# Mixture-of-experts tiles of seven sequences in one queue, with blocks that wait until they are full

## The reference, cut to what matters

```python
m = _layernorm(x, ln2_g, ln2_b)                     # x: 4096 tokens x 128
probs = softmax(m @ Wg)                             # E = 8 experts
wts, idx = top_k(probs, 2); wts = wts / sum(wts)
h1 = gelu(einsum('td,edf->etf', m, W1) + b1)        # F = 512
ye = einsum('etf,efd->etd', h1, W2) + b2
out = x + sum_k wts[k] * ye[idx[k]]                 # each token uses 2 of 8 experts
```

## Time and profile before

| | us |
|---|---|
| timed runs, three | 1022.54, 1027.51 (median), 1029.69 |
| span of the profiled execution, first to last instruction | 987.7 |
| the profiled execution's own time | not given; the median stands for it |
| PE busy | 820.5 (83%) |
| VectorE busy | 665.6 (67%) |
| ScalarE busy | 600.2 (61%) |
| GpSimd busy | 424.9 (43%) |

### The profile page before, as it was taken

One profiled execution on the slowest core, in us unless ns is written; L12 is line 12 of the kernel. 1 busy time (PEld: TensorE's weight loads), 2 busy tenths in 40 slices (PEclk: granted clock), 3 DMA queues, 4 the chain that ended last, 5 costly groups with the idle time before them and its releaser, 6 DMA issues. The chain is left out here.

```text
span 987.7 us, 15981 instructions
## 1 busy us (share of the span) xinstructions
PE 820.5 (83%) x5416; PEld 516.9 (52%) x5416; DVE 665.6 (67%) x1341; ACT 600.2 (61%) x1016; POOL 424.9 (43%) x543
## 2 busy tenths in 40 slices
PE   3558898878898999788989998988898888898772
PEld 1444445434555654345556555654565555478771
DVE  4538858886879688868886878687867576223112
ACT  2123446644787687447876887677768876556341
POOL 5544333534553455464534553454556013115263
PEclk9675798888899999898999999998999998699797
DMA  6500321991522300015233321053223320558793
GB/s 196 169 12 9 122 98 49 292 347 45 179 90 89 101 21 9 12 33 180 89 100 103 108 86 57 30 183 97 89 80 123 119 80 27 181 188 298 236 309 95
DMA packets 106286, 116.77 MB, mean 118 GB/s; under 512 B 7983, under 2 KB 89310, under 8 KB 106206
## 3 DMA queue, kind: packets, MB, share of 16 engines
q1 hardware_dynamic: 102110, 107.36, 34.3%
q0 software_dynamic: 4096, 8.40, 2.6%
HBM read 77.24 MB, written 38.49 MB: 117 GB/s over the span
## 5 line engine op out<-in xcount | busy, mean ns | idle before, releaser
L1456 DVE TENSOR_REDUCE QA<-psB 128x2 f32<-128x1024 f32 x256 | 311.9, 1219 | 124.0 <-PE psB L1143 121.7
L943 ACT ACTIVATE PT<-psB 128x1024 f32<-128x1024 f32 x256 | 261.9, 1023 | 134.3 <-PE psB L1159 130.4
L1159 PE MATMUL psB<-Q,KT 32*128 32x512 f32 x512 | 134.4, 521 | 34.0 <-ACT PT L943 20.6
L1143 PE MATMUL psB<-KT,Q 24*128 24x512 f32 x512 | 136.9, 530 | 22.6 <-DVE QA L1456 21.7
L1171 PE MATMUL psV<-PT,VA 128*32 128x512 f32 x1024 | 148.5, 654 | 0.6
L1236 PE MATMUL psA<-MX,WB 128*128 128x128 f32 x792 | 109.4, 290 | 31.2 <-ACT H L971 19.7
L971 ACT ACTIVATE H<-psA,WB 128x128 f32<-128x128 f32 x396 | 109.8, 376 | 33.3 <-PE psA L1236 31.3
L1236 PEld LDWEIGHTS psA<-MX,WB 128*128 128x128 f32 x792 | 100.0, 202 | 39.4 <-issue 28.3
L1246 PEld LDWEIGHTS psY<-WB,H 128*128 128x128 f32 x792 | 96.8, 194 | 27.8 <-ACT H L971 16.8
L1159 PEld LDWEIGHTS psB<-Q,KT 32*128 32x128 f32 x512 | 49.7, 191 | 117.1 <-ACT PT L943 75.3
L1246 PE MATMUL psY<-WB,H 128*128 128x128 f32 x792 | 107.6, 282 | 0.0
(11 more groups left out here) (198 smaller groups left out, 1360.0 us busy)
## 6 DMA issues: line engine op xcount, KB each, us to landing
WB<-w_rows SPq DMA_DIRECT2D x99, 578.0 KB, 5.7
pairs<-XT SPq DMA_DIRECT2D x2, 5120.0 KB, 18.5
outs<-XT SPq DMA_DIRECT2D x2, 5120.0 KB, 33.5
XT<-pairs SPq DMA_DIRECT2D x99, 64.0 KB
outs<-YT SPq DMA_DIRECT2D x99, 64.0 KB
w_rows<-WB SPq DMA_DIRECT2D x8, 578.0 KB, 3.3
X<-in_L_attn_x_dram SPq DMA_DIRECT2D x8, 256.0 KB, 3.0
H<-in_L_ffn_W_dram SPq DMA_DIRECT2D x8, 256.0 KB, 3.9
```

What stands on the lines that cost most here:

```text
L943: act.activation(PT[:, (c % 2) * G + j:(c % 2) * G + j + 2, :], psT, ACT.Exp, scale=SCALE).then_inc(t_taken.sem, 1)
L1143: pe.matmul(dst[:, h, :], chunk(Q1[r, g, :], c), KT[r, g, :], start=True, stop=True).then_inc(s_full.sem, 1)
L1159: pe.matmul(psT[:, h, :], chunk(KT[r, g, :], c), Q2[r, g % 2, :], start=True, stop=True).then_inc(t_full.sem, 1)
L1456: dve.tensor_reduce(QA[:, c, g * G + j:g * G + j + 2, RM], plain(b, i), AX_X, ALU.max).then_inc(s_taken.sem, 1)
```

## The change

- Elements 0 to 6 form one group and element 7 the other. A group has *stages*: after each element from the second on, a stage runs the tiles whose blocks are full for certain (128 rows); unfilled blocks wait for later elements, and the last stage of a group takes all that is left. Seven stages with 9, 8, 8, 8, 8, 22, 15 tiles: 78 instead of 99. Windows: 3, 3, 3, 3, 3, 8, 5.
- Stages begin at slots 88, 120, 152, 184, 216, 248, 280. Windows start 8 slots apart, in the last two stages 4 apart (248 to 276 and 280 to 296); there the third W1 step stands half a slot later.
- `tile_map` looks at up to 224 blocks, keeps the flags of the stage before and takes the difference; 10 instructions (8 or 9 in a group's first stage) instead of 6; it runs after elements 1 to 7.
- A row in `XS` has 130 columns. The scatter writes 129 of them, with the pair's place in the result at one end. VectorE reads it back from the loaded tile (`tile_places`, slot 4 of a window) and waits there until the store of the window before last has landed.
- The result is stored straight in token order (`TK`), by GpSimd with an indirect DMA a tile, at slot 11 of a window. The gathers go. SyncE fetches the results of an element in two plain DMAs of 256 KB into one buffer for each choice, each once the combine before has freed it.
- Combines and output stores of elements 0 to 6 all come behind the last window of their group: fetches at slots 288, 290, ... 300, combines at 290, 292, ... 302; element 7 at 308 and 310. The sum X1 + Z1 is kept in XZ, which now holds eight elements.
- `XS` is cleared in eight pieces, one a turn, with 17 MB in all; four areas with 20.5 MB were cleared before. `YS` needs no clearing.

```diff
-    MEMBERS = [[0]] + [[b, b + 1] for b in range(1, B - 1, 2)] + [[B - 1]]
+    MEMBERS = [list(range(B - 1)), [B - 1]]
...
+            known = 2 * T // TW * (i + 1) + (E - 1 if b == m[-1] else 1 - E)
+            if i or b == m[-1]:
+                STAGE[b] = len(TILES)
+                TILES.append(known - given)
...
-        STRIDE = [8, 8, 8, 5, 8]
+        STRIDE = [8] * (STAGES - 2) + [4, 4]
...
             def rows_in(w):
...
                 if w >= 2:
                     u = use(members(w - 2)[0], "x")
                     sp.wait_ge(u.taken, u.after)
+                    sp.wait_ge(places.sem, places.at(w - 2, 1))
...
+            def fetch_rows(b):
+                if b == MEMBERS[GROUP_OF[b]][0]:
+                    for w in range(LAST_WINDOW[GROUP_OF[b]] - 1, LAST_WINDOW[GROUP_OF[b]] + 1):
+                        sp.wait_ge(y_out[w % 2], moved(w))
+                for k in range(2):
+                    if b > 0:
+                        sp.wait_ge(*((combined.sem, combined.at(b - 1, 1)) if k else (dve_y, b)))
+                    first = (k * B + b) * T
+                    sp.dma_start(YG[:, k, :, :], TK[first:first + T, :].rearrange("(c p) n -> p c n", p=P)).then_inc(fetched[k], 16)
...
-            TILE = {3: (tile_step(0, next_rows),), 7: (tile_step(0, next_weights),), 9: (tile_step(0, rows_out),)}
+            TILE = {3: (tile_step(0, next_rows),), 7: (tile_step(0, next_weights),)}
+            END = {4: (fetch(0),), 6: (fetch(1),), 8: (fetch(2), keep(0),), 10: (fetch(3), keep(1),), 12: (fetch(4), keep(2),),
+                   14: (fetch(5), keep(3),), 16: (fetch(6), keep(4),), 18: (keep(5),), 20: (keep(6),)}
...
-                            pool.indirect_dma_start(XS[GROUP_OF[b] % 2], bass.IndirectOffsetOnAxis(IDX[:, b % 6, k, c:c + 1], 0),
-                                                    ZM[:, b % 2, c, :], None).then_inc(scattered[k][c], 16)
+                            pool.indirect_dma_start(XS.rearrange("r n -> (r n)").unsqueeze(1), bass.IndirectOffsetOnAxis(IDX[:, b % 2, k, c:c + 1], 0),
+                                                    ZM[:, b % 2, c, k:k + C + 1], None).then_inc(scattered[k][c], 16)
...
+            def tile_out(first):
+                w = window(first)
+                pool.wait_ge(places.sem, places.at(w, 1))
+                pool.wait_ge(y_taken.sem, y_taken.at(w, 1))
+                for i in range(len(members(w))):
+                    pool.indirect_dma_start(TK, bass.IndirectOffsetOnAxis(IDT[:, w % 2, i:i + 1], 0),
+                                            YT[:, w % 2, i, :], None).then_inc(y_out[w % 2], 16)
+
+            TILE = {11: (tile_step(0, tile_out),)}
...
             POST = {6: (c_norm,), 16: (positions, scatter(0),), 21: (scatter(2),)}
-            END = {4: (gather(0, 0),), 8: (gather(0, 1), gather(0, 2),), 16: (gather(0, 3),), 17: (gather(1, 0),),
-                   31: (gather(1, 1),), 32: (gather(1, 2), gather(1, 3),)}
...
+            def tile_places(first):
+                w, size = window(first), len(members(window(first)))
+                dve.wait_ge(xt_in[w % 2], moved(w))
+                if w >= 2:
+                    dve.wait_ge(y_out[w % 2], moved(w - 2))
+                own_p.begin(w)
+                own_p.link(dve.tensor_tensor(IDF[:, 0:size], XT[:, w % 2, 0:size, 0], XT[:, w % 2, 0:size, C + 1], ALU.min))
+                own_p.end()
+                dve.tensor_tensor(IDT[:, w % 2, 0:size], IDF[:, 0:size], AWAY[:, w % 2, 0:size], ALU.min).then_inc(places.sem, 1)
...
-            TILE = {10: (tile_step(0, tile_out),)}
+            TILE = {4: (tile_step(0, tile_places),), 10: (tile_step(0, tile_out),)}
...
-            END = {30: (combine(0),), 46: (combine(1),)}
+            END = {6: (combine(0),), 8: (combine(1),), 10: (combine(2),), 12: (combine(3),), 14: (combine(4),), 16: (combine(5),),
+                   18: (combine(6),)}
```

More of the change, by code:

```diff
@@ L421, in build @@
         scattered = [[sem(f"scattered_{k}_{c}") for c in range(NT)] for k in range(2)]
-        gathered = [[sem(f"gathered_{k}_{c}") for c in range(NT)] for k in range(2)]
+        ids_ready = sig("ids_ready")
+        places = sig("places")
+        fetched = sem("fetched_0"), sem("fetched_1")
         combined = sig("combined")
@@ L465, in __call__, with tiles @@
                 self.step(n, *self.parts)
-        def tiles(n, at, table):
+        def tiles(n, at, table, end_table=None):
             for w, start in enumerate(START):
-                for step in table.get(SLOTS * n + at - start, ()):
+                now = end_table if end_table and window_stage(w) >= STAGES - 2 else table
+                for step in now.get(SLOTS * n + at - start, ()):
                     if step.which < len(members(w)):
@@ L576, in next_weights, with fetch, step @@
                     weights_in(window(n) + 2)
-            def rows_out(n):
-                window_out(window(n))
+            def fetch_rows(b):
[7 more added lines that the diff above has]
+                    sp.dma_start(YG[:, k, :, :], TK[first:first + T, :].rearrange("(c p) n -> p c n", p=P)).then_inc(fetched[k], 16)
+            def fetch(which):
+                def step(group):
+                    if which < len(MEMBERS[group]):
+                        fetch_rows(MEMBERS[group][which])
+                return step
             def store(b):
@@ L1207, in rank @@
                 for back in range(NT + 1):
-                    last = pe.matmul(dst[:, 0:(NT + 1) * E], ones[:, :] if back else lower[:, :],
+                    last = pe.matmul(dst[:, 0:(NT + 1) * E], ones[:, 0:P] if back else lower[:, :],
                                      SEL[:, NT - back:2 * NT + 1 - back, :].rearrange("p c e -> p (c e)"),
@@ L1536, in c_rank @@
             def c_rank(b):
-                i = MEMBERS[GROUP_OF[b]].index(b)
-                if i:
+                group = GROUP_OF[b]
+                first = b == MEMBERS[group][0]
+                if not first:
                     dve.wait_ge(use(b - 1, "rank").taken, use(b - 1, "rank").after)
@@ L1561, in tile_map, with by_block @@
-                dve.tensor_tensor(TMAP[:, group % 2:group % 2 + 1], MF[:, :], TD[:, :], ALU.add).then_inc(map_ready.sem, 1)
-                own_t.end()
+                stage, group = STAGE[b], GROUP_OF[b]
+                blocks = BLOCKS_OF[group]
+                first, last = stage == STAGE_GROUP.index(group), b == MEMBERS[group][-1]
+                def by_block(v):
+                    return v[:, 0:E * blocks].rearrange("p (e j) -> p e j", j=blocks)
+                new, old, place_of = TF[:, stage % 2, :], TF[:, (stage + 1) % 2, :], TO[:, :]
@@ new lines, in tile_map @@
+                starts = TH[:, :].rearrange("p (e j) -> p e j", j=NB)[:, :, BLOCK_0[group]:BLOCK_0[group] + blocks]
+                own_t.begin(stage)
+                dve.wait_ge(use(b, "rank").taken, use(b, "rank").after)
+                count = POS[:, b % 2, NT, :].unsqueeze(2).to_broadcast([P, E, blocks])
+                own_t.link(dve.scalar_tensor_tensor(out=by_block(new), in0=count, scalar=0.0 if last else 1.0 - TW, in1=starts,
+                                                    op0=ALU.add, op1=ALU.is_gt))
@@ new lines, in tile_map @@
+                added = new
+                if not first:
+                    dve.tensor_tensor(by_block(old), by_block(new), by_block(old), ALU.subtract).then_inc(dve_n, 1)
+                    dve.wait_ge(dve_n, stage - group)
+                    added = old
+                own_t.link(dve.tensor_tensor_scan(by_block(place_of).rearrange("p e j -> p (e j)"), ones[:, 0:E * blocks],
+                                                  by_block(added).rearrange("p e j -> p (e j)"), 0.0, ALU.mult, ALU.add))
```

261 lines of the change are left out of this document (126 added, 135 removed).

## The result

The changed kernel takes 1059.45 us (median of 4 runs, 1053.98 to 1062.14) against 1025.03 us (1019.91 to 1029.69) for the kernel before on the same chip: a ratio of 1.0386, interval 1.0319 to 1.0454. I had forecast 1087, range 1045 to 1118. Slower was right; the number is 28 us too high, and further down it turns out that two errors partly cancel in it. That the time lies in the range is in part luck: as a difference I had forecast 59.5 us, and this comparison gave 34.4.

What follows compares the result with a forecast made beforehand. Dropping windows was taken to save nothing inside the turns; behind them only windows, the last gate and combines overlap. 15 + 23.5 + 23 - 2 = 59.5 us on the median 1027.51 gave 1087 us, range 1045 to 1118.

Steps and rivals of the forecast that it cites:

- The base: Starting time: span 987.7 us, median 1027.51 taken for the profiled execution, the 39.8 us outside the span staying.
- Removed tiles: 20 expert tiles fewer inside turns 1 to 7, where a window was priced at nothing: 0 us.
- Removed gathers: Gathers on GpSimd in the first 8 slots of turn 6 go: -4 us, bounds 0 and -4.1.
- Stores on GpSimd inside the turns: Scatters of a window's three tiles delay norm_2 and ZA by 3.4 us in turns 3 to 6: +13.6 us.
- The longer map: VectorE's tile map takes 3.8 us instead of 1.6, half the further 2.2 us let through: +5.5 us, 0 to 12.
- The gate against the stores: Behind the turns, element 7's gate waits for store landings: rank 20 us later, its windows' first copy +23.5 us.
- The combines in the last five windows: Seven combines between the last window copies wait for fetches, gaps 17, 17, 17 and 5: +23 us, lower bound +8.
- fetches slip past: Rival, chance 0.12: fetches land in about 3 us and the gate loses less, 1052 us.
- The end: From the last window copy to the last combine, 13.8 us instead of 15.5: about -2 us.
- Waits behind the turns alone: Rival, chance 0.2: the turns absorb the stores in the missing fourth window's TensorE time, 1072 us.
- nothing comes of it: Rival, chance 0.04: gain and loss cancel, 1027 us.
- Turns bound by TensorE: Rival, chance 0.1: 20 removed tiles give back 2.2 us each, 44 us in the turns, 1003 us in all.

Runs made afterwards that it cites:

- e1: Kernel before with the 20 expert tiles inside the turns left out and nothing put in their place: 990.72 us against 981.07, ratio 1.0094.
- e11: Changed kernel with the edits of e2, e3 and e4, third window of turns 2 to 6 started at slot 16, not 8: 1024.13 us, ratio 1.0403.
- e9: Changed kernel with 24 idle TensorE matmuls where the fourth window is missing, third quarter of turns 2 to 6: 1060.3 us, ratio 1.0769.
- e5: Changed kernel run again as it is, beside the kernel before on one chip: 1054.23 us against 982.95, ratio 1.071.
- e6: Changed kernel with nine more unused VectorE instructions of 224 columns behind each tile map in turns 2 to 7: 1081.56 us, ratio 1.0984.
- e4: Changed kernel with the second window's store one slot earlier and the third's four slots later inside the turns: 1044.32 us, ratio 1.0602.
- e3: Changed kernel with four result buffers instead of two for the windows of the last two stages: 1038.23 us, ratio 1.0544.
- e2: Changed kernel with a second result buffer and the fetches queued ahead of the weights: 1040.72 us, ratio 1.0574.

## Why the prediction came out as it did

**The base.** The step that failed is "what lies outside the span (1027.51 - 987.7 = 39.8 us) stay". Outside the span there are 1.8 us (1060.68 - 1058.9), and 1.7 or 1.8 in every other run. So the trace shown came from an execution of some 989 us, the median from runs of 1023 to 1030; that the two were on different chips is not on record, but the two kinds of comparison above make it likely. The forecast for the span was 1047 and 1058.9 was measured: 12 too low. The 1087 is 28 too high because 38 us were added that lie outside no span.

**Removed tiles.** About right at 0, though as a sum: in e1 missing windows gave back some 3 us in three quarters, and gathers that moved took some 8 us. The stretch of turn 1 on which I based the 0 was a weak witness, since it also had 199 GB/s of DMA for 101 in turn 4. In the third quarter the price is 0: see e1's 27.7 us without a window or a gather, and e11, which restored the window and the clock and gained nothing. The 3 to 6 us that the expectation of e9 gives to the clock are what e1's two longer quarters show, and these hold gathers.

**Removed gathers**, -4 predicted: the first quarter of turn 6 went from 28.2 to 24.1 us. Two more in the third quarter of turn 3, 438.58 and 439.87, I had missed.

**Stores on GpSimd inside the turns**, 13.6 predicted: the place was right (in front of rsA, then ZA), the size too large. Undoing it gave 7.9 us in the quarters and 9.9 in the median. The term that was mis-sized is the number of stores: in turns 4 to 6 the third window has two tiles and not three (654.97 and 656.23). In turn 3, where it has three, the wait of ZA grew by 3.3 us in e5 (predicted 3.4), in turns 4 to 6 by 1.2 to 2.0.

**The longer map**, 5.5 predicted: duration right (3.66 for 3.8), cover wrong. By e6 3.55 us more cost 5.3 a turn, 1.5 for one. The map grew by some 2 us in turns 3 and 5 and is new in 2, 4 and 6 (3.66); at 1.5 for what exceeds the 1.6 us that were covered that is 3.1 us a turn. With the stores out of the way (e4) the quarters of turns 4 and 5 are 3.2 and 3.3 us longer than before, and 12 us longer over turns 2 to 6 (less the two gathers of turn 3), which with the stores' 7.9 makes up the 19.9 us between e5 and the kernel before. So the term of 5.5 us was less than half of what came. Between the first traces turns 0 to 7 differ by +0.9, -3.3, +4.6, +7.2, +7.6, +2.9, +0.3 and +5.0 us (in turn 6 the gathers go as well), +25.2 in all where I had 15. The failed step is "most of 1.6 us is covered; of the further 2.2 us I let half through". Two turns that are 0.3 us apart told me about a map of 1.6 us, not about one that outlasts its cover.

**The gate against the stores**, 23.5 predicted, 30.2 measured. The rank came 20.6 us later against the first copy (943.57 - 891.10 = 52.5, before 31.9): predicted 20. The order on GpSimd was as written, on its timeline:

```profile
949.90 0.96 POOL L826 DMA_INDIRECT pairs<-ZM,IDX  x1 [0.30 <-issue]
951.16 0.97 POOL L835 DMA_INDIRECT results<-YT,IDT  x1 [0.30 <-issue]
...
954.96 0.96 POOL L826 DMA_INDIRECT pairs<-ZM,IDX  x1 [0.30 <-issue]
```

The first window of element 7 got its weights at 968.87, 25.3 us behind the rank, where I had 25. What was mis-sized is the last step, "from their issue to the copy it is 12.4": it took 19.1. VectorE first had to take the positions of another window, at 976.94 after 8.40 us of waiting for a store, and only behind them comes the copy of the one-tile window, which frees psY for TensorE. In the working the landing of a store (4 us) is counted six times at one place (10 less at 2.2) and comes to 9 less at 2.15 at another, while the steps written out hold it five times; measured were 2.3 without weights on the way and 5.0 to 6.4 with them. In e3 no store ends a wait and the stretch to this copy is 12.3 us shorter, 8.4 of them ahead of the rank; but from the issue of the weights (949.58) to the copy (965.61) it still takes 16.0 us, with VectorE waiting 8.23 us for rows. So stores account for the smaller part of that last step; the rest was not traced.

**The combines in the last five windows**, 23 predicted, 23.8 measured, gaps of 17.7, 16.9, 16.6 and 5.7 for 17, 17, 17 and 5. SyncE's issues show the order: three weights, three rows, then the fetches, whose second half waits for the combine.

```profile
988.84 1.69 SPq L578 DMA_DIRECT2D WB<-w_rows  x3
991.96 2.55 SPq L569 DMA_DIRECT2D XT<-pairs  x3
994.62 7.08 SPq L599 DMA_DIRECT2D YG<-results  x4
```

The first combine started at 999.00, 11.05 us behind the copy, where I had 9: the rows stand between, which I had left out. The second fetch's first half was issued at 1000.2 and used at 1003.05, 4.05 us behind the first combine, where I had 5. That 17 came out is partly luck: I had the fetch issued some 2.4 us behind the copy and then queued for 6.6; it was issued 6.7 us behind it and used 4.4 later. Most of the wait is SyncE's order of issue, with rows in it, and not the queue of landed weights. The rival "fetches slip past" had its premise, a median landing of 2.9 us over all fetches, and still fell, because the first fetch is issued 5.8 us after the weights. The rule of the Trainium skill ("DMA: Bandwidth & Descriptors", section on queues, rings and completion order) that descriptors of one queue are consumed in ring order fits with it: it took 4.4 us from the issue at 994.62 to the combine with weights and rows ahead, 2.9 as median. No run here isolates the rule: e2, which takes the fetches out from behind the weights and gained 13.5, adds a buffer as well.

**The end**, -2 predicted, -4.1 measured.

**The rivals.** "Waits behind the turns alone" falls by the table's first row, "nothing comes of it" by the ratio of the result. "Turns bound by TensorE" falls by e1.

## What to carry to other kernels

Work taken from an engine that is busy 90% of a stretch can be worth nothing when the stretch is a ring of four engines, and a few microseconds in front of the ring's narrow places cost what they take or more: GpSimd's 1 us scatters before a norm passed through one for one, VectorE's longer map at 1.5 for one. Before a slower clock is blamed for a stretch, count the instructions of the small engines in it: in e1 gathers that had moved looked like the price of a missing window. When a step is moved to a queue, write down the queue's whole order around the place and ask which of its entries others wait for: that gave the two largest terms here within 30%. Before adding anything to a median, compare the profiled execution with it: if the two differ, a forecast is best given as a difference and as two totals.

## What the runs showed of the hardware

- A scatter of 64 KB by an indirect DMA landed 2.3 us after its start when no weights were on the way (953.70 to 956.03, 962.53 to 964.85) and 5.0 to 6.4 us when they were (919.64 to 924.65, 894.96 to 901.33). I had taken 4 for all.
- In the third quarters of the changed kernel TensorE's granted clock has a mean of 0.62 to 0.83, so 1.2 GHz for part of them; in turn 5 of e5 it is 1.00 up to the wait for ZA at 650.45 and 0.58 to 0.77 from there to 671.83. 24 idle matmuls brought the mean of that quarter only from 0.79 to 0.86. In the kernel before the third quarter of turn 1, without a window and at a clock of 0.81, takes 27.4 us, that of turn 5, with a window and at 1.00, 27.6: there the lower clock cost no time.
- One and the same kernel took 981 to 985 us in three comparisons and 1023 to 1025 in two, with a mean clock of 0.91 to 0.92 in the former and 0.89 in the one of the latter for which it is on record, while the changed kernel took 1054 and 1059 us, 0.5% apart.
